# Two chained attention layers on one core: convolutions in idle score banks, six chunks of x loaded at once, and the next image's projection spread over layer 1

## The reference

```
# layer 0, per image: x is 256 x 4096
q, k, v = Wq x + bq, Wk x + bk, Wv x + bv      # q, k: 32 x 4096; v: 256 x 4096
attn    = softmax(q^T k, over i)               # 4096 x 4096
x1      = gamma * (v attn) + x
# layer 1: theta = 32 x 4096; phi, g are max-pooled 2x2 to 1024 positions
energy  = theta^T phi                          # 4096 x 1024
out     = g softmax(energy, over j)^T          # 128 x 4096
y       = gamma * (out_w out + out_b) + x1
```

## Time and profile before

| | |
|---|---|
| median of 3 runs | 2952.17 us (2945.66 to 2953.29) |
| profiled execution, its own time | 2952.56 us |
| its span | 2950.8 us |
| mean granted TensorE clock | 0.967 |
| busy: PE, DVE, POOL, ACT | 2757.0, 2008.1, 1949.9, 1750.7 us |
| chain that ended last | PE 77%, issue 9%, DVE 5%, ACT 5%, POOL 4%, DMA 1% |

### The profile page before, as it was taken

The page is one execution under the profiler, slowest core; times in us unless marked ns, Lnnn a source line. Parts: engine busy times, 40 slices in busy tenths (PEclk is TensorE's granted clock), DMA queues, the critical chain, the costliest instruction groups (busy, mean ns, idle before and its releaser), DMA issues.

```text
span 2950.8 us, 39091 instructions
## 1 busy us (share of the span) xinstructions
PE 2757.0 (93%) x12260; PEld 2180.1 (74%) x12260; DVE 2008.1 (68%) x3303; ACT 1750.7 (59%) x3171; POOL 1949.9 (66%) x1480
## 2 busy tenths in 40 slices
PE   5899999989999999998999999999799999999978
PEld 4677777766677777776667777777666777777756
DVE  4577767756767677675776776777576767777665
ACT  3455565555665655555676565565566556555657
POOL 2366666765676667764677677666567766666658
PEclk7799999998999999999899999999999999999989
DMA  2000000011210000001120000000111000000011
GB/s 88 22 15 15 15 15 15 22 36 36 72 50 15 15 15 22 22 15 36 51 68 34 15 22 22 15 15 15 44 58 58 23 21 15 15 15 15 15 35 65
DMA packets 44280, 87.10 MB, mean 30 GB/s; under 512 B 2736, under 2 KB 2864, under 8 KB 44080
## 3 DMA queue, kind: packets, MB, share of 16 engines
q1 hardware_dynamic: 35360, 68.17, 6.8%
q10 hardware_dynamic: 8720, 16.46, 1.9%
HBM read 51.06 MB, written 33.55 MB: 29 GB/s over the span
## 4 chain that ended last, share of the span: by engine, by line
PE 77%; issue 9%; DVE 5%; ACT 5%; POOL 4%; DMA 1%; POOLq 0%; ACTq 0%; DVEq 0%
PE o_ps L797 30%; PE o_ps L775 16%; PE s_ps L765 8%; PE aux L828 8%; POOL prob_l L427 3%; PE aux L808 3%; PE aux L841 2%; ACT prob_h L490 2%; DVE mx L650 2%; PE aux L837 2%; PE aux L845 1%; PE aux L812 1%; PE aux L862 1%; PE o_ps L828 1%; PE o_ps L862 1%
## 5 line engine op out<-in xcount | busy, mean ns | idle before, releaser
L427 POOL TENSOR_TENSOR prob_l<-prob,prob_h 128x512 fp32r<-128x512 f32 x1280 | 1639.7, 1289 | 751.6 <-ACT prob_h L490 744.2
L487 ACT ACTIVATE prob<-s_ps 128x512 f32<-128x512 f32 x1280 | 768.5, 600 | 974.2 <-PE s_ps L765 973.5
L650 DVE TENSOR_REDUCE mx<-aux 128x1 f32<-128x512 f32 x1115 | 769.5, 690 | 459.3 <-PE aux L828 458.0
L797 PE MATMUL o_ps<-prob_h,vh 128*128 128x512 f32 x2304 | 935.8, 406 | 17.5 <-issue 12.6
L797 PE MATMUL o_ps<-prob_h,vl 128*128 128x512 f32 x2304 | 904.6, 393 | 0.0
L612 DVE TENSOR_TENSOR acc<-prob,acc 128x512 f32<-128x512 f32 x1216 | 836.1, 688 | 45.4 <-ACT prob L487 34.2
L775 PE MATMUL o_ps<-prob_l,vh 128*128 128x512 f32 x2304 | 756.0, 400 | 37.4 <-POOL prob_l L427 37.0
L490 ACT ACTIVATE prob_h<-s_ps 128x512 fp32r<-128x512 f32 x1280 | 762.1, 595 | 0.0
L775 PEld LDWEIGHTS o_ps<-prob_l,vh 128*128 128x128 f32 x2304 | 437.4, 191 | 144.7 <-POOL prob_l L427 57.0
L797 PEld LDWEIGHTS o_ps<-prob_h,vh 128*128 128x128 f32 x2304 | 437.0, 190 | 124.3 <-issue 24.8
L765 PE MATMUL s_ps<-queries,keys 128*128 128x512 f32 x1280 | 509.2, 399 | 0.8 <-DVE queries L669 0.8
(11 more groups left out here) (91 smaller groups left out, 1997.9 us busy)
## 6 DMA issues: line engine op xcount, KB each, us to landing
xa<-x SPq DMA_DIRECT2D x32, 512.0 KB, 3.7
spill<-xa SPq DMA_DIRECT2D x32, 512.0 KB, 2.7
xa<-spill SPq DMA_DIRECT2D x32, 512.0 KB, 3.6
y<-xa SPq DMA_DIRECT2D x32, 512.0 KB, 2.8
xp<-x ACTq DMA_DIRECT2D x30, 512.0 KB, 3.7
xp<-x SPq DMA_DIRECT2D x2, 512.0 KB, 5.8
...
```

Of the source, the lines that this page charges most:

```text
L427: nc.gpsimd.tensor_tensor(out=prob_l[:, i, :], in0=prob[:, i, :], in1=prob_h[:, i, :].bitcast(f32), op=ALU.subtract).then_inc(pl_ready, 1)
L487: nc.scalar.activation(prob[:, i, :], s_ps[s][:, :], ACT.Exp).then_inc(p_ready, 1)
L650: ins = nc.vector.tensor_reduce(out=dst, in_=bank[:, :], axis=AX.X, op=ALU.max)
L797: last = mm(o_ps[ct][:, :], value(parts, l, t, ct), prob_h[:, h % RING, :], start=t == 0 and parts is vh, stop=False)
```

## The change

In `BEFORE` lists, where no attention runs, jobs may now use all eight banks: `S0` to `S2` (`s_ps`), `O0` (`o_ps[0]`) and `A` (`acc`) are added. The first image's convolutions go round five banks and its maxima round three. At the start SyncE issues six loads of x, four into `xa` (where the addition later finds them, so that these four are not loaded again) and two into `xp`; ACT's loads begin with chunk 6. The rounding `X` of a chunk stands two chunks ahead. Ahead of layer 1 three chunks of the next image are projected and not four; the four maxima of layer 1's second chunk move into its first chunk's tiles; `XB` of the last chunk moves into layer 0. The projection of chunk 3 stands in layer 1's chunk 0, and those of chunks 4 to 7 in twelve places, two a chunk, in chunks 1 to 6. In layer 1's own convolutions `K1` comes before `G1`, and its queries (`K1Q`) are made apart from its keys (`K1K`, `K1M`), so that maxima wait for the keys alone.

```diff
-X0, X1, Y = range(3)
+X0, X1, Y, S0, S1, S2, O0, A = range(8)
...
+    turn = [X1, Y, S0, S1, S2]
+    st_turn = [X0, O0, A]
+    begin = [Job("X", 0, 0, 0, 0), Job("X", 0, 0, 1, 0)]
     for c in range(NCH):
-        first.append(Job("X", 0, 0, c, 0))
-    lists = []
-    for c in range(NCH):
-        k, v0, v1 = project0(0, c, (X1, Y, X0 if c == 0 else Y))
-        if c == 0:
-            lists += [first[0], first[1], k, Job("K0L", 0, 0, 0, 0), v0, Job("V0L", 0, 0, 0, 0),
-                      v1, Job("V0L", 0, 0, 0, 1)]
-        else:
-            if c + 1 < NCH:
-                lists.append(first[c + 1])
-            st = [maxima(0, 0, 0, c - 1, s, X0) for s in range(SUBS)]
-            lists += [st[0], k, st[1], v0, Job("K0L", 0, 0, c, 0), st[2], Job("V0L", 0, 0, c, 0), v1, st[3],
-                      Job("V0L", 0, 0, c, 1)]
-    lists += [maxima(0, 0, 0, NCH - 1, s, X0 if s % 2 == 0 else X1) for s in range(SUBS)]
-    lists.append(on(Job("M", 0, 0, 0, 0), X0))
-    before[0] = lists
+        k, kl, v0, vl0, v1, vl1 = project0(0, c, [turn[(3 * c + i) % len(turn)] for i in range(3)])
+        st = [maxima(0, 0, 0, c - 1, s, st_turn[(4 * c + s) % 3]) for s in range(SUBS)] if c else []
+        begin += st[:2] + [k, v0, kl] + st[2:] + [vl0, v1, vl1]
+        if c + 2 < NCH:
+            begin.append(Job("X", 0, 0, c + 2, 0))
+    begin += [maxima(0, 0, 0, NCH - 1, s, (X0, O0, A, X1)[s]) for s in range(SUBS)]
+    begin.append(on(Job("M", 0, 0, 0, 0), X0))
+    before[0] = begin
...
-                    put(g + 7, 1, Job("X", 1, b, c, 0))
-                    put(g + 10, 1, on(Job("G1", 1, b, c, 0), X1))
-                    put(g + 13, 1, on(Job("K1", 1, b, c, 0), X1))
-                    put(g + 14, 1, Job("K1K", 1, b, c, 0))
-                    put(g + 15, 1, Job("K1L", 1, b, c, 0))
-                    put(g + 17, 1, on(Job("T1", 1, b, c, 0), X1))
-                    put(g + 18, 1, Job("T1L", 1, b, c, 0))
+                    put(g + 6, 1, Job("X", 1, b, c, 0))
+                    put(g + 10, 1, on(Job("K1", 1, b, c, 0), X1))
+                    put(g + 11, 1, Job("K1K", 1, b, c, 0), Job("K1Q", 1, b, c, 0))
+                    put(g + 12, 1, Job("K1M", 1, b, c, 0), Job("K1L", 1, b, c, 0))
+                    put(g + 14, 1, on(Job("G1", 1, b, c, 0), X1))
+                    put(g + 16, 1, on(Job("T1", 1, b, c, 0), X1))
+                    put(g + 17, 1, Job("T1L", 1, b, c, 0))
...
+                put(g + 22, 1, Job("XB", 0, b, n, 0))
                 if more:
                     put(g + 21, 1, Job("X", 0, b + 1, 0, 0))
-                    put(g + 27, 1, Job("X", 0, b + 1, 1, 0))
-
-        last = (0, b, NCH - 1)
+                    put(g + 26, 1, Job("X", 0, b + 1, 1, 0))
...
+        k1, g1 = on(Job("K1", 1, b, c, 0), X0), on(Job("G1", 1, b, c, 0), S0)
+        t1 = on(Job("T1", 1, b, c, 0), S0)
+        st = [maxima(1, b, 0, 1, s, (X1, Y, S1, S2)[s]) for s in range(SUBS)]
+        m0 = on(Job("M", 1, b, 0, 0), X1)
+        add, rnd = Job("N", *last, 0), Job("X", 1, b, c, 0)
+        k1k, k1q, k1m, k1l = (Job(name, 1, b, c, 0) for name in ("K1K", "K1Q", "K1M", "K1L"))
+        t1l = Job("T1L", 1, b, c, 0)
...
+            k0, k0l, v00, v00l, v01, v01l = project0(b + 1, 0, (X1, Y, S0))
+            k1_, k1_l, v10, v10l, v11, v11l = project0(b + 1, 1, (S1, S2, X1))
+            k2, k2l, v20, v20l, v21, v21l = project0(b + 1, 2, (O0, Y, S1))
+            before[tile_no(1, b, 0)] = [
+                d1, k0, d2, v00, add, v01, rnd, k0l, v00l, v01l, k1_, v10, k1_l, v10l, v11, v11l,
+                k1, Job("X", 0, b + 1, 2, 0), k1k, g1, k1m, t1, *st, k2, m0, k1q, k1l, t1l, v20, k2l, v20l, v21, v21l,
+                Job("X", 0, b + 1, 3, 0)]
         else:
-            before[tile_no(1, b, 0)] = chain1 + chain2 + chain3 + st[0] + [m0] + st[1]
+            before[tile_no(1, b, 0)] = [d1, d2, add, rnd, k1, k1k, g1, k1m, t1, *st, m0, k1q, k1l, t1l]
...
+                if n in (3, 4):
+                    for i in range(2):
+                        put(g + 3 + 2 * i, 3, maxima(1, b, NCH - 1, 0, 2 * (n - 3) + i, X0))
             else:
                 for s in range(SUBS):
-                    put(g + 2 + s, 3, maxima(1, b, NCH - 1, 0, s, X0))
-            if n + 1 < NCH:
-                put(g + 1, 1, on(Job("M", 1, b, n + 1, 0), Y))
-            if more:
-                for s, (t, at) in enumerate(((0, X1), (0, Y), (2, Y), (3, Y)) if n < NCH - 1 else
-                                            ((0, X1), (0, Y), (1, X1), (1, Y))):
-                    put(g + t, 3, maxima(0, b + 1, 0, n, s, at))
-                c = n + 3
-                if n >= 1 and c < NCH:
-                    k, v0, v1 = project0(b + 1, c, (X1, X1, X1))
-                    put(g + 1, 1, k)
-                    put(g + 3, 1, Job("K0L", 0, b + 1, c, 0))
-                    put(g + 4, 1, v0)
-                    put(g + 5, 1, Job("V0L", 0, b + 1, c, 0))
-                    put(g + 6, 1, v1)
-                    put(g + 7, 1, Job("V0L", 0, b + 1, c, 1))
-                    if c + 1 < NCH:
-                        put(g + 7, 1, Job("X", 0, b + 1, c + 1, 0))
-                if n == NCH - 1:
-                    put(g + 4, 1, on(Job("M", 0, b + 1, 0, 0), Y))
+                    put(g + s, 1, maxima(1, b, 1, 1, s, X0))
+                put(g + 4, 1, on(Job("M", 1, b, 1, 0), X0))
...
+            if more:
+                if n < NCH - 1:
+                    for s, (t, place, at) in enumerate(((0, 1, X1), (2, 3, Y), (3, 3, Y), (4, 1, X1))):
+                        put(g + t, place, maxima(0, b + 1, 0, n, s, at))
+                else:
+                    for s in range(SUBS):
+                        put(g + s // 2, 1, maxima(0, b + 1, 0, n, s, (X1, Y)[s % 2]))
+                    put(g + 4, 1, on(Job("M", 0, b + 1, 0, 0), Y))
+        if more:
+            g = tile_no(1, b, 0)
+            k, kl, v0, vl0, v1, vl1 = project0(b + 1, 3, (X1, X1, X1))
+            put(g + 1, 1, k)
+            put(g + 2, 1, kl)
+            put(g + 4, 3, v0)
+            put(g + 5, 1, vl0)
+            put(g + 6, 1, v1)
+            put(g + 7, 1, vl1)
+            places = [(8 * n + t) for n in range(1, 7) for t in (1, 5)]
+            for c in range(4, NCH):
+                k, kl, v0, vl0, v1, vl1 = project0(b + 1, c, (X1, X1, X1))
+                at = places[3 * (c - 4):3 * (c - 3)]
+                put(g + at[0], 3, k)
+                put(g + at[0] + 2, 1, kl)
+                put(g + at[1], 3, v0)
+                put(g + at[1] + 2, 1, vl0)
+                put(g + at[2], 3, v1)
+                put(g + at[2] + 2, 1, vl1)
+            for c, t in ((4, 5), (5, 8 + 6), (6, 24 + 3), (7, 32 + 4)):
+                put(g + t, 1, Job("X", 0, b + 1, c, 0))
...
-        LAST_READ.append(Job("K1", 1, _job.b, _job.c, 0) if _job.l else Job("V0", 0, _job.b, _job.c, 1))
-    if _job.name in ("K0", "V0", "K1", "K1K", "T1"):
+        LAST_READ.append(Job("G1", 1, _job.b, _job.c, 0) if _job.l else Job("V0", 0, _job.b, _job.c, 1))
+    if _job.name in ("K0", "V0", "K1Q", "K1K", "T1"):
         HIGH[_job] = len(HIGH)
...
+for _g, _jobs in BEFORE.items():
+    for _job in _jobs:
+        if _job in BANK and BANK[_job] >= S0:
+            LAST_ON[_g, BANK[_job]] = _job
...
-        aux = (pb("aux0"), pb("aux1"), o_ps[1])
+        aux = (pb("aux0"), pb("aux1"), o_ps[1], *s_ps, o_ps[0], acc)
...
+        def x_of(b, c):
+
+            p = image0(b, c)
+            if p < ASLOTS:
+                return xa[p], xa_in[p], 16
+            p -= ASLOTS
+            return xp[p % PSLOTS], xp_in[p % PSLOTS], 16 * (p // PSLOTS + 1)
 
...
-            for p in range(PSLOTS):
+            for p in range(ASLOTS + PSLOTS):
                 load_p(p)
-            for n in range(ASLOTS):
-                load_a(0, 0, n)
             for k in range(B * 2 * NCH):
                 l, b, n = k // NCH % 2, k // (2 * NCH), k % NCH
...
+                    if image0(b, c) < ASLOTS:
+
+                        act.wait_ge(xl_ready, ROUND[Job("X", 0, 0, c, 0)] + 1)
...
-                elif name in ("K0", "K1"):
+                elif name in ("K0", "K1Q"):
                     q = queries[:, q_slot(l, b, c), :]
+                    if l:
+                        job = Job("K1", 1, b, c, 0)
+                        bank = aux[BANK[job]]
                     wait_full(act, job)
...
+                    if k == 1 and ASLOTS + PSLOTS <= p < B * NCH:
...
+                    if (h, A) in LAST_ON:
+                        wait_free(dve, LAST_ON[h, A])
...
+                elif name == "K1M":
+                    at = slice(c * P, (c + 1) * P)
+                    dve.wait_ge(high_ready, HIGH[Job("K1K", 1, b, c, 0)] + 1)
+                    dve.wait_ge(ppool_ready, image0(b, c) + 1)
+                    low(keys[1][LK, at], ppool[K1, :], cols[K1, COL_KQ[1]:COL_KQ[1] + 1],
+                        keys[1][K1, at]).then_inc(key1_ready, 1)
...
```

(45 more changed lines are left out.)

56 lines of the change are left out of this document (23 added, 33 removed).

## The result

The changed kernel takes 2877.74 us (median of 4 runs, 2876.71 to 2878.19); the kernel before took 2948.91 us beside it. The ratio is 0.9761, with a 95% interval of 0.9738 to 0.9784: faster by 71 us, where 106 were forecast. That is inside the range of 2806 to 2892 us and outside the forecast's own of 2820 to 2872. The profiled execution has a span of 2875.7 us, 75.1 less than before.

A forecast was written before the change was run, and what follows sets the result against it. Outside layer 0, where PE is busy 97% at full clock, waits and low clock were taken to bound the stages. Terms -36 - 42 - 10 - 18 = -106 against 2952.6 gave 2846 us, range 2806 to 2892, the forecast's own 2820 to 2872.

The forecast's parts named there:

- First projection, -36: First image's projection ahead of layer 0: 115.1 us now, first accumulation at 79 us after; bounds -16 to -40.
- the 6.5: First projection: us taken for one chunk's period, between 5.7 and 10.4 by the share of low clock.
- The sentence that put the load on the path: First projection: a 3.65 us load of x is in the chain of waits that repeats every 12.7 us.
- Lists, -42: Lists ahead of layer 1, images 0 to 2: -14 us each, 41.8 to 28; bounds -8 to -17 each.
- The walk: List ahead of layer 1, followed from D1 to the first accumulation: 25 us, before 3 us added for low clock.
- Last list, -10: List ahead of layer 1 for the last image: 20.6 us for 30.6; bounds -5 to -12.
- Layer 0, 0: Layer 0's 28 chunks of 66.4 us: no change, with +-8 us.
- the rival of a wait in every chunk: Layer 0: ACT and DVE late together, maxima on X0 hold PE; 2972 us at 4.5 us a chunk; chance 0.02.
- Layer 1, -18: Layer 1 with the next image's projection: -6 us each for three images, 144.3 against 150.0; bounds -14 to +4.
- from 17.4 to 19.7: Layer 1's chunk 0, in us: it becomes DVE's, with K0L and V0L adding 2.9 us of DVE work.
- Layer 1 gives nothing back: Layer 1: slots share bank X1 with maxima, so it stays at 150 or goes to 156; 2864 to 2882 us; chance 0.15.
- The low clock stays: First projection, lists and layer 1: low clock remains although the work is denser; 2907 us; chance 0.09.

The follow-up runs named there:

- The fill: The changed kernel with 12 matmuls of 512 columns that nothing reads, issued where PE waits ahead of layer 1's first scores: 2873.9 us.
- e12: The changed kernel, but each K0 inside layer 1 has only 32 of 512 columns evacuated on ScalarE and VectorE: 2848.6 us.
- e13: The changed kernel with only 32 of 512 columns evacuated of each K0 and each V0 inside layer 1: 2853.1 us.

## Why the prediction held, and where it did not

*First projection, -36: right, -40.8.* The period came to 6.3 us where 6.5 was taken, with K0L, maximum, K0 and evacuations in the loop as walked; the chain of waits of the changed kernel:

```profile
29.68 0.75 DVE queries L649
...
31.69 0.92 PE s_ps L835 x4
...
33.81 0.68 ACT queries L525
...
35.98 0.75 DVE queries L649
```

The two periods with ScalarE's own loads took 3.0 us more together, where 4 had been taken. From the last K0L to the first accumulation it was 9.1 us where 8.5 were summed, and the 3 to 4 us added there for low clock were not needed. The reason given for the 6.5 was wrong, that PE had the full clock wherever it was busy over 80%: layer 1 in the earlier trace rows has PE busy 139.86 of 150.70 us at 0.90. The sentence that put the load on the path was half right: it was on it, but worth 1.7 us a period and not 3.65.

*Lists, -42: right, -48.3.* The walk gave 25 us and the lists took 24.8 to 26.2; the 3 us added for low clock were not needed, since these lists ran at 1.00. *Last list, -10: right, -9.2. Layer 0, 0: right*, within 0.2 us in each image, so the regrouped K1 and G1 and the rival of a wait in every chunk are out.

*Layer 1, -18: wrong, +21.8,* and outside its own bounds of -14 to +4 an image (it was +7.3). Two terms of this step were mis-sized. The first is the low clock. The step took 2 us an image for it. The mean clock of 0.91 over 156.6 us is 14 us of lost clock, as much as before (0.90 of 150.7); where PE isn't the bound, not all of it is lost time. The step gave no reason why the spread schedule should keep the clock up. The fill shows that one wait of PE, of 2.4 to 2.9 us, brings low clock; that the waits of 1 to 2 us inside the chunks do so too is argued from `e12`, where three of them and the low clock shrank together. The spread schedule has waits of 1.0 to 1.85 us in chunks 0, 2, 3, 4 and 6 of the first image. The second is the evacuation of a K0. The step counted 1 us of wait for each, for the one maximum that shares its bank, and that it replaced an equal one. The wait on that bank was 0.38 us once; the waits stood elsewhere. The kernel with small K0 evacuations shows 9.5 us an image for five of them, waits and the low clock behind them together. So it is mainly the order of work on the engines, and not the bank X1: 2.0 us on ScalarE and then 1.5 on VectorE are ahead of exponentials, maxima and sums, and whatever PE wants next comes late. In chunk 0, where VectorE has no room, the projection of chunk 3 costs 6.9 us at full clock and 10.3 as it ran, where the step, from 17.4 to 19.7, had given it 2.3.

How much of the 13 us an image is clock and how much is lateness can't be split exactly, since one can bring the other. In chunk 0 of image 1 it is 3.4 (25.6 against 22.2 at full clock) and 2.5 (22.2 against 19.7). In `e12` 9.5 went with the K0 evacuations.

*The rivals.* "Layer 1 gives nothing back" (0.15) is what happened, for the reason that it named only in part: its price of 2864 to 2882 us holds the measured time. Its bank was wrong, and there is luck in the price: layer 1 took 157.3 us, more than the 150 to 156 it is made of, and the 11 us gained elsewhere cover that. With the other terms as forecast, layer 1 would have made it about 2886 us. "The low clock stays" holds for layer 1 and for the last list (0.65): the first projection ran at 0.94 and the other lists at 1.00. The rule of the Trainium skill's page "TensorE: Matmul & The Clock Gate", section "A second HAM failure mode: psum-queue depth-cycling", that a kernel that goes round banks idles between groups often enough for the clock to swing, did not show in these stages. The rule of the same page of the Trainium skill, section "What's actually happening", that activity releases the low clock, is what the filled wait shows: in image 1's chunk 0, 0.75 to 1.00 by twelve matmuls that nothing reads.

What stays open: why the low clock comes after some waits of 1 to 2 us and not after others of the same length (chunk 1 of image 0 ran at 1.00, chunk 1 of image 1 at 0.85, with nearly the same order). It is also open which of the two engines' parts of the evacuation costs more, and where the last 4 us of `e13`'s layer 1 are. Whether a cheaper form of the K0 evacuation exists that computes all of it wasn't tried.
